# A graph network's edge loads: one transfer for each batch of a chunk, in place of one for the whole chunk

## The chip, the cores and the metric

The kernel runs on 1 core of a Trainium2 chip. The metric is the device time of one execution in microseconds; lower is better. Engines are named as in the profile: PE is TensorE (matmul), PEld its weight load, DVE is VectorE, ACT is ScalarE, POOL is GpSimd, SP is SyncE, which here only issues transfers.

## What is computed

Two layers of a graph network on 12,500 nodes of 128 features, with 200,000 edges sorted by their target node `dst`. Each layer normalizes x, sums edge attributes by target node, and adds the outcome of small dense products to x. The first layer sums 64 attributes of an edge and divides by the number of edges of the node; the second sums 128.

```python
h = jnp.maximum(_layernorm(x, axis=-1), 0.0)
# layer 0, edge_attr_64
edge_projected = edge_attr @ W_edge.T
aggregated = jax.ops.segment_sum(edge_projected, dst, num_segments=num_nodes)
aggregated = aggregated / jnp.clip(degree, 1.0)[:, None]
x = x + jnp.concatenate([h @ W_self.T, aggregated @ W_neigh.T], axis=1) @ W_final.T + b_final
h = jnp.maximum(_layernorm(x, axis=-1), 0.0)
# layer 1, edge_attr_128
agg = jax.ops.segment_sum(edge_attr, col, num_segments=x.shape[0])
x = x + jax.nn.relu(jnp.concatenate([h, agg], axis=1) @ W1 + b1) @ W2 + b2
```

## The kernel before

The edges are cut into 128 chunks of 13 x 128 (the first 32) or 12 x 128 edges (the last chunk, 127, has 832). The sum by target node is done by TensorE: for each unit of 128 edges DVE builds a one-hot matrix of 128 edges by 64 nodes (a window of nodes), and matmuls multiply the edges' attributes by it. `ring128` holds the 128 attributes of the edges, `ring64` the 64. Since `dst` is sorted and low nodes have more edges, late chunks cover more nodes than one window; so a chunk has 1, 2, 3 or 4 batches, each with a window of its own: `PARTS = (1, 2, 3, 4)` batches of `RUNS = (13, 6, 4, 3)` units, by quarter of the chunk numbers. Within a batch of R units, partition p holds R neighbouring edges, so a partition's run is R x 512 B in `ring128` and R x 256 B in `ring64`.

The work goes in ticks t = 0 to 127, one chunk each, with dense work for groups of 512 nodes between. `ORDER` lists the chunk of each tick. Chunks 15 to 20 come first. Then one from the high end (127, 126, ...) and one from the low end (21, 22, ...) take turns until tick 112. Chunks 0 to 14 come last. So two-batch chunks (32 to 63) and three-batch chunks meet four-batch chunks (96 to 127) in the middle of the run. By the order of the ticks: even ticks 6 to 68 have four batches (the first of them, chunk 127, two and a short one), odd ticks 7 to 27 one and 29 to 91 two, even ticks 70 to 92 three, ticks 93 to 112 three, and the last 15 one.

Loads go into a ring of `SLOTS = 5` slots, all of them issued by SP in the order of the ticks. SP issues the load of tick t once PE has finished the matmuls of tick t-5 (semaphore `s_mm`); PE waits at the start of tick t until the whole chunk is in the slot (semaphore `s_load[slot]`, whose target is the table `LOADED`), and for the one-hots and for free accumulators. Each transfer raises `s_load` by 16. Chunk t's last matmul is that of line 671, on which SP's waits are recorded. ACT issues the loads of x and the stores of the result on its own queue.

Of the kernel before, what the change touches and what calls it, by code (L numbers as in the profile page):

```python
# [14 lines left out]
P = 128  # L15
# [9 lines left out]
PARTS = (1, 2, 3, 4)  # L25
CH = 128
# [8 lines left out]
SLOTS = 5  # L35
# [22 lines left out]
def run_of(c):  # L58
    return RUNS[c // 32]


def first_edge(c):
    return c * 13 * P if c <= 32 else 32 * 13 * P + (c - 32) * 12 * P


def batches_of(c):


    q = c // 32
    if c == CH - 1:  # L70
        return [(0, 3, P, 0), (3, 3, P, 1), (6, 1, H, 0)]
    kinds = ((2,), (0, 1), (0, 1, 2), (0, 1, 0, 1))[q]
    return [(b * RUNS[q], RUNS[q], P, kinds[b]) for b in range(PARTS[q])]


def build_gnn(nc, x, dst, edge_attr_128, edge_attr_64, W_self, W_neigh, W_edge, W_final, b_final,
# [77 lines left out]
    for q, g in enumerate(SEQ):  # L154
        for at, other in ((FIRST_W, g + 4 if g and g in LOWER else 0), (UPPER_AT, g - 4 if g in UPPER else 0)):
            if other in (LOWER if at == FIRST_W else UPPER) and other:
                a = at + (g - 1) % 4 * GW
# [46 lines left out]
    for q in range(NG - 1, -1, -1):  # L204
        t = min(NEIGH[q] - 9, SELF[0] - 2 if SELF else CH)
# [11 lines left out]
    HOT_SUMS, ADDED, LOADED, in_slot = [0], [0], [], [0] * SLOTS  # L217
    for t, c in enumerate(ORDER):
        HOT_SUMS.append(HOT_SUMS[-1] + (2 if c >= 96 else 3))
        ADDED.append(ADDED[-1] + len(batches_of(c)))  # L220
        in_slot[t % SLOTS] += 64 if c == CH - 1 else 32
        LOADED.append(in_slot[t % SLOTS])


# [31 lines left out]
    with ExitStack() as ctx:  # L256
# [3 lines left out]
        def sem(name):  # L260
            return ctx.enter_context(nc.semaphore(name))
# [88 lines left out]
        s_load = [sem(f"s_load{i}") for i in range(SLOTS)]  # L350
# [22 lines left out]
        def otherwise(eng, general):  # L373

            eng.wait_ge(s_gen, 1)
            again = eng.value_load(gen[0:1, 0:1], min_val=0, max_val=1)
            with eng.If(again > 0):
                general()

        def every_group(eng, group):  # L380
            with eng.Fori(0, GG - 1) as g:
                group(g)
            group(GG - 1)
# [5 lines left out]
        @block.sync  # L389
        def _(sp):  # L390
            sp.wait_ge(s_dst_clear, 1)
            z0 = 32 * UNITS * P
            sp.dma_start(dst_i[0:32, :], dst[0:z0].rearrange("(r e) -> r e", r=32)).then_inc(s_dst0, 16)

            def load_edges(t):
                c = ORDER[t]
                slot, e0, R = t % SLOTS, first_edge(c), run_of(c)
                if t >= SLOTS:
                    sp.wait_ge(s_mm, t - SLOTS + 1)
                nb = 2 if c == CH - 1 else PARTS[c // 32]  # L400
                e1 = e0 + nb * R * P
                for ring, feats in ((ring128, edge_attr_128), (ring64, edge_attr_64)):
                    sp.dma_start(ring[:, slot, 0:nb * R, :].rearrange("p (b r) f -> p b (r f)", b=nb),
                                 feats[e0:e1, :].rearrange("(b p r) f -> p b (r f)", p=P, r=R)).then_inc(s_load[slot], 16)
                    if c == CH - 1:
                        sp.dma_start(ring[0:H, slot, 6, :], feats[e1:E, :]).then_inc(s_load[slot], 16)

            load_edges(0)
            for r0, r1, e0, w in ((96, 126, first_edge(96), 12 * P), (126, 127, first_edge(126), 12 * P),
                                  (127, 128, first_edge(127), LAST_E), (32, 96, z0, 12 * P)):  # L410
                sp.dma_start(dst_i[r0:r1, 0:w], dst[e0:e0 + (r1 - r0) * w].rearrange("(r e) -> r e", e=w)).then_inc(s_dst, 16)
            rest = 12 * P - LAST_E
            sp.dma_start(dst_i[127:128, LAST_E:12 * P], dst[E - rest:E].rearrange("(r e) -> r e", r=1)).then_inc(s_dst, 16)
            for t in range(1, CH):
                load_edges(t)
            sp.wait_ge(s_store, 16 * (NG + 1))

            def general():
                sp.dma_start(gen_dst_i, dst.rearrange("(p e) -> p e", p=GP)).then_inc(s_gdst, 16)

                def group(g):
                    with sp.Fori(0, PASSES) as w:
                        with sp.Fori(0, GC) as c:
                            sp.wait_ge(s_gmm, (g * PASSES + w) * GC + c + 1)
                            for ring, feats in ((gen_r128, edge_attr_128), (gen_r64, edge_attr_64)):
                                sp.dma_start(ring, feats.rearrange("(p c r) f -> p c (r f)", p=GP, r=GR)[
                                    :, bass.ds(c, 1), :].rearrange("p o f -> p (o f)")).then_inc(s_gload, 16)
                    sp.wait_ge(s_gst, g * 32 + 32)
                    if not isinstance(g, int):
                        rows = x[bass.ds(g * GW, GW), :].rearrange("(j p) f -> p j f", p=P)  # L430
                        sp.dma_start(x0[:, 0:2, :], rows[:, 0:2, :]).then_inc(s_gx, 16)
                        sp.dma_start(x0[:, 2:4, :], rows[:, 2:4, :]).then_inc(s_gx, 16)
                        sp.wait_ge(s_gstep, g * GSTEPS + GSTEPS + 1)
                        rows = out[bass.ds(g * GW, GW), :].rearrange("(j p) f -> p j f", p=P)
                        sp.dma_start(rows[:, 0:2, :], x0[:, 0:2, :]).then_inc(s_gst, 16)
                        sp.dma_start(rows[:, 2:4, :], x0[:, 2:4, :]).then_inc(s_gst, 16)
                    else:
                        n0 = g * GW
                        sp.dma_start(x0[:, 0, :], x[n0:n0 + P, :]).then_inc(s_gx, 16)
                        sp.dma_start(x0[0:LAST_N, 1, :], x[n0 + P:N, :]).then_inc(s_gx, 16)  # L440
                        sp.wait_ge(s_gstep, g * GSTEPS + GSTEPS + 1)
                        sp.dma_start(out[n0:n0 + P, :], x0[:, 0, :]).then_inc(s_gst, 16)
                        sp.dma_start(out[n0 + P:N, :], x0[0:LAST_N, 1, :]).then_inc(s_gst, 16)
                        sp.wait_ge(s_gst, g * 32 + 64)

                every_group(sp, group)

            otherwise(sp, general)
# [928 lines left out]
```

## Time and profile before

| | |
|---|---|
| runs | 531.97, 534.71, 535.15 us, median 534.71 |
| the profiled execution | 538.03 us, of which 536.2 us are the span of its instructions |
| PE, PEld busy | 494.8 us (92%), 440.6 us (82%) |
| DVE, POOL, ACT busy | 416.8, 382.9, 178.5 us |
| moved by the DMA engines | 169.55 MB, 316 GB/s on average |
| mean granted clock of TensorE | 0.978 |

The profile is of one execution of its own, so sums on it are made against 538.03 us, and the difference of the span, 1.8 us, lies outside the first and the last instruction. Busy times are shares of the span. A DMA share is that of the 16 engines, and can pass 1 where the times of packets overlap.

### The profile page before, as it was taken

What the parts mean: (1) busy time and instruction counts of PE and PEld (TensorE: products, weight loads), DVE (VectorE), ACT (ScalarE), POOL (GpSimd) and SP (SyncE); (2) the same over time, 40 slices, a digit from 0 to 9 for tenths busy, and PEclk for the clock granted to TensorE, in tenths of its full rate; (3) what the DMA queues carried; (4) which work ended last, traced back from release to release, by engine and by line L of the source; (5) the groups of instructions that cost most, each with busy time, mean ns of one, the idle gap of its engine ahead of it and who ended that gap; (6) DMA issues with size and microseconds to landing.
All of it is one profiled execution on the core that took longest, in us unless ns stands there. A gap on an engine that the chain in (4) does not pass through costs nothing.

```text
span 536.2 us, 26042 instructions
## 1 busy us (share of the span) xinstructions
PE 494.8 (92%) x10913; PEld 440.6 (82%) x10913; DVE 416.8 (78%) x1403; ACT 178.5 (33%) x397; POOL 382.9 (71%) x523
## 2 busy tenths in 40 slices
PE   8999788899989989989999999999999899999995
PEld 7889788798867878878887888789787788888784
DVE  5848989779994769978899679989969789956422
ACT  0011024243524234542525242534433362312201
POOL 2799586878696764897778977697975585863820
PEclk9997999999997989999999999999999899999998
DMA  8998999999995999999999999999999899987801
GB/s 280 398 363 293 377 372 353 364 325 363 334 329 188 343 345 299 361 312 321 368 343 381 300 343 328 377 322 316 366 339 326 278 337 325 315 306 264 335 23 33
DMA packets 113231, 169.55 MB, mean 316 GB/s; under 512 B 5486, under 2 KB 84310, under 8 KB 113111
## 3 DMA queue, kind: packets, MB, share of 16 engines
q1 hardware_dynamic: 85843, 154.42, 82.3%
q10 hardware_dynamic: 27268, 13.43, 8.7%
q8 instruction: 88, 1.44, 1.1%
q14 instruction: 32, 0.26, 0.1%
HBM read 161.43 MB, written 6.40 MB: 313 GB/s over the span
## 4 chain that ended last, share of the span: by engine, by line
PE 75%; DVE 10%; issue 9%; POOL 4%; DVEq 1%; ACT 0%; ACTq 0%; POOLq 0%
PE ps L644 25%; PE ps L662 14%; PE ps L646 5%; PE ps L731 5%; PE ps L710 5%; PE ps L722 4%; PE ps L691 4%; PE ps L682 4%; PE ps L724 3%; DVE agg L1080 2%; DVE onehot L1050 2%; POOL hot_sum L530 2%; POOL hot_part L530 1%; PE ps L583 1%; PE ps L596 1%
## 5 line engine op out<-in xcount | busy, mean ns | idle before, releaser
L644 PEld LDWEIGHTS ps<-onehot,ring 128*64 128x64 f32 x3126 | 194.6, 139 | 32.0 <-issue 25.6
L644 PE MATMUL ps<-onehot,ring 128*64 128x64 f32 x3126 | 213.3, 225 | 6.9 <-issue 6.3
L646 PE MATMUL ps<-onehot,ring 128*64 128x64 f32 x3126 | 213.8, 225 | 6.3 <-issue 6.1
L646 PEld LDWEIGHTS ps<-onehot,ring 128*64 128x64 f32 x3126 | 194.8, 139 | 7.6 <-issue 7.6
L530 POOL TENSOR_TENSOR hot_part<-onehot 128x384 bf16<-128x384 f32 (+2 forms) x128 | 118.0, 922 | 113.9 <-DVE onehot L1050 110.9
L1050 DVE TENSOR_TENSOR onehot<-iota_win,rel 128x384 f32<-128x384 f32 (+3 forms) x192 | 168.8, 880 | 0.2
L1080 DVE TENSOR_TENSOR agg<-ps,agg 128x128 f32 (+1 forms) x319 | 94.8, 297 | 85.2 <-PE ps L671 61.0
L662 PE MATMUL ps<-onehot,ring 128*64 128x64 f32 x3126 | 120.4, 224 | 7.6 <-issue 7.4
L662 PEld LDWEIGHTS ps<-onehot,ring 128*64 128x64 f32 x3126 | 107.9, 140 | 7.7 <-issue 7.4
L530 POOL TENSOR_TENSOR hot_sum<-hot_part 128x128 bf16<-128x128 bf16 x96 | 52.9, 551 | 7.5
L897 ACT ACTIVATE hn<-x,nmr,rstd 128x128 f32<-128x128 f32 x98 | 40.3, 483 | 19.9 <-DVE nmr L1142 19.9
L952 ACT ACTIVATE hid<-ps,b_col 128x512 f32<-128x512 f32 (+1 forms) x25 | 16.9, 678 | 90.0 <-PE ps L724 90.0
L508 POOL TENSOR_TENSOR x<-x,b_bc 128x512 f32<-128x512 f32 (+1 forms) x25 | 33.8, 1352 | 13.2 <-ACT h L937 13.2
L937 ACT ACTIVATE h<-x,nmr,rstd 128x128 f32<-128x128 f32 x98 | 40.4, 484 | 7.8 <-DVE nmr L1194 7.7
L731 PE MATMUL ps<-w,hid 128*128 128x128 f32 x196 | 30.4, 300 | 8.2 <-ACT own L912 5.7
L530 POOL TENSOR_TENSOR hot_sum<-hot_sum,hot_part 128x128 bf16<-128x128 bf16 x64 | 34.3, 536 | 5.0
L516 POOL MEMSET agg<- 128x1536 f32 (+2 forms) x26 | 35.4, 1364 | 2.7 <-PE ps L724 2.7
L495 POOL TENSOR_TENSOR x<-x,b_bc 128x512 f32<-128x512 f32 (+1 forms) x25 | 37.1, 1485 | 0.0
L912 ACT COPY own<-ps 128x512 f32<-128x512 f32 (+1 forms) x25 | 14.4, 577 | 64.2 <-PE ps L691 47.4
L731 PEld LDWEIGHTS ps<-w,hid 128*128 128x128 f32 x196 | 25.5, 202 | 10.2 <-issue 7.8
L710 PEld LDWEIGHTS ps<-w_c,agg 128*128 128x128 f32 x248 | 31.0, 196 | 3.1 <-issue 2.9
L502 POOL TENSOR_TENSOR x<-x,own 128x512 f32<-128x512 f32 (+1 forms) x25 | 33.5, 1339 | 0.0
(127 smaller groups left out, 648.5 us busy)
## 6 DMA issues: line engine op xcount, KB each, us to landing
ring<-in_edge_attr_dram SPq DMA_DIRECT2D x95, 768.0 KB, 5.5
ring<-in_edge_attr_dram SPq DMA_DIRECT2D x96, 384.0 KB, 7.1
ring<-in_edge_attr_dram SPq DMA_DIRECT2D x32, 832.0 KB, 5.9
ring<-in_edge_attr_dram SPq DMA_DIRECT2D x32, 416.0 KB, 7.6
x<-in_x_dram ACTq DMA_DIRECT2D x23, 256.0 KB, 7.1
out_dram<-x ACTq DMA_DIRECT2D x23, 256.0 KB
x<-in_dst_dram SPq DMA_DIRECT2D x1, 384.0 KB
x<-in_dst_dram SPq DMA_DIRECT2D x1, 208.0 KB, 3.5
```

What stands on the lines that cost most here:

```text
L495: nc.gpsimd.tensor_tensor(rows, rows, b0_bc[:, :].unsqueeze(1).to_broadcast([P, nt, D]), ALU.add).then_inc(s_xb, 1)
L516: nc.gpsimd.memset(agg[:, :, a:b], 0.0).then_inc(s_zero, 1)
L530: nc.gpsimd.tensor_tensor(out, a, b, ALU.add).then_inc(s_hotsum, 1)
L644: nc.tensor.matmul(bank[0:H, o:o + WIN], ring128[0:K, slot, u, 0:H], hots, start=u == 0, stop=r == R - 1, skip_group_check=True)
L646: nc.tensor.matmul(bank[H:P, o:o + WIN], ring128[0:K, slot, u, H:D], hots, start=u == 0, stop=r == R - 1, skip_group_check=True)
L662: nc.tensor.matmul(bank[feats, o:o + WIN], ring64[0:K, slot, u, :], onehot[0:K, hot, u, :], start=False, stop=True, skip_group_check=True)
L710: last = nc.tensor.matmul(ps_nb[:, j // 2, j % 2, :], agg[:, 1 + k, a + j * P:a + (j + 1) * P], w_c[:, k, :], start=i == 0, stop=i == len( ...
L731: last = nc.tensor.matmul(ps_row[:, j * D:(j + 1) * D], hid[:, j * P:(j + 1) * P], w2[:], start=True, stop=True)
L897: last = nc.scalar.activation(hn[:, j, :], x0[:, j0 + j, :], ACT.Relu, bias=nmr1[:, u, j:j + 1], scale=rstd1[:, u, j:j + 1])
L937: last = nc.scalar.activation(h2[:, j, :], x0[:, j0 + j, :], ACT.Relu, bias=nmr2[:, u, j:j + 1], scale=rstd2[:, u, j:j + 1])
L1050: made = nc.vector.tensor_tensor(onehot[:, t % HOTS, a:b, :], iota_win[:, :].unsqueeze(1).to_broadcast([P, b - a, WIN]), rel[:, c // 32, a ...
L1080: nc.vector.tensor_tensor(here, ps[:, t % BANKS, o:o + w * WIN].rearrange("p (a n) -> p a n", a=w), here, ALU.add).then_inc(s_added, 1)
```

## The change

`load_edges` used to issue one transfer for each of the two rings of a chunk, whose access pattern went over the partition, the batch and the run. Now it issues one for each batch. Each covers 128 partitions by one run. The runs and their places are the same, and so are the bytes. The targets of `s_load` grow with the count of transfers. Nothing is changed on PE, DVE, ACT or POOL: PE still waits for the whole chunk.

```diff
     for t, c in enumerate(ORDER):
         HOT_SUMS.append(HOT_SUMS[-1] + (2 if c >= 96 else 3))
         ADDED.append(ADDED[-1] + len(batches_of(c)))
-        in_slot[t % SLOTS] += 64 if c == CH - 1 else 32
+        in_slot[t % SLOTS] += 32 * (3 if c == CH - 1 else PARTS[c // 32])
         LOADED.append(in_slot[t % SLOTS])
...
                 e1 = e0 + nb * R * P
                 for ring, feats in ((ring128, edge_attr_128), (ring64, edge_attr_64)):
-                    sp.dma_start(ring[:, slot, 0:nb * R, :].rearrange("p (b r) f -> p b (r f)", b=nb),
-                                 feats[e0:e1, :].rearrange("(b p r) f -> p b (r f)", p=P, r=R)).then_inc(s_load[slot], 16)
+                    for b in range(nb):
+                        a = e0 + b * R * P
+                        sp.dma_start(ring[:, slot, b * R:(b + 1) * R, :].rearrange("p r f -> p (r f)"),
+                                     feats[a:a + R * P, :].rearrange("(p r) f -> p (r f)", p=P, r=R)).then_inc(s_load[slot], 16)
                     if c == CH - 1:
                         sp.dma_start(ring[0:H, slot, 6, :], feats[e1:E, :]).then_inc(s_load[slot], 16)
```

SP's instructions in the middle of the run, for a chunk of four batches, one of two, and the first load of the next one of four (the sizes are partitions, batches and elements of a run), before:

```order
L403 DMA ring128<-in_edge_attr_128_dram 128x4x384
L403 DMA ring64<-in_edge_attr_64_dram 128x4x192
L403 DMA ring128<-in_edge_attr_128_dram 128x2x768
L403 DMA ring64<-in_edge_attr_64_dram 128x2x384
L403 DMA ring128<-in_edge_attr_128_dram 128x4x384
```

and now:

```order
L405 DMA ring128<-in_edge_attr_128_dram 128x384 x4
L405 DMA ring64<-in_edge_attr_64_dram 128x192 x4
L405 DMA ring128<-in_edge_attr_128_dram 128x768 x2
L405 DMA ring64<-in_edge_attr_64_dram 128x384 x2
L405 DMA ring128<-in_edge_attr_128_dram 128x384 x4
```

Each transfer over several batches has become as many transfers in a row, at the same place in SP's order, behind the same wait for the slot. At the start, SP's instructions for chunk 127, chunk 21 and the first load of chunk 126, before:

```order
L403 DMA ring128<-in_edge_attr_128_dram 128x2x384
L406 DMA ring128<-in_edge_attr_128_dram 64x128
L403 DMA ring64<-in_edge_attr_64_dram 128x2x192
L406 DMA ring64<-in_edge_attr_64_dram 64x64
L403 DMA ring128<-in_edge_attr_128_dram 128x1664
L403 DMA ring64<-in_edge_attr_64_dram 128x832
L403 DMA ring128<-in_edge_attr_128_dram 128x4x384
```

and now:

```order
L405 DMA ring128<-in_edge_attr_128_dram 128x384 x2
L408 DMA ring128<-in_edge_attr_128_dram 64x128
L405 DMA ring64<-in_edge_attr_64_dram 128x192 x2
L408 DMA ring64<-in_edge_attr_64_dram 64x64
L405 DMA ring128<-in_edge_attr_128_dram 128x1664
L405 DMA ring64<-in_edge_attr_64_dram 128x832
L405 DMA ring128<-in_edge_attr_128_dram 128x384 x4
```

The chunks of one batch keep their two transfers. The other engines have the same instructions in the same order.

## Rows read from the trace of the kernel before

**Rows 1.** The page: span, busy time of engines, busy tenths by slice.

```profile
span 536.2 us, 26042 instructions
PE 494.8 (92%) x10913; PEld 440.6 (82%) x10913; DVE 416.8 (78%) x1403; ACT 178.5 (33%) x397; POOL 382.9 (71%) x523
PE   8999788899989989989999999999999899999995
```

**Rows 2.** The page: the chain that ended last, by engine.

```profile
PE 75%; DVE 10%; issue 9%; POOL 4%; DVEq 1%; ACT 0%; ACTq 0%; POOLq 0%
```

**Rows 3.** Waits of all engines: us in total, times, longest us.

```profile
POOL hot_part L530 <- DVE onehot L1050: 110.9, 78, 9.1
ACT hid L952 <- PE ps L724: 90.0, 24, 10.7
DVE agg L1080 <- PE ps L671: 61.0, 46, 4.6
...
PEld ps L644 <- issue: 25.6, 61, 2.8
...
PEld ps L724 <- issue: 12.0, 48, 0.5
```

**Rows 4.** Waits of SP over the run, same columns.

```profile
SPq L403 <- PE ps L671: 367.6, 123, 10.8
```

**Rows 5.** Timeline of SP, 5 to 9.2 us: start, us, what.

```profile
5.32 3.97 SPq L403 DMA_DIRECT2D ring<-in_edge_attr_dram  x8
```

**Rows 6.** The page: issues of loads onto the ring, KB each, us to landing.

```profile
ring<-in_edge_attr_dram SPq DMA_DIRECT2D x95, 768.0 KB, 5.5
ring<-in_edge_attr_dram SPq DMA_DIRECT2D x96, 384.0 KB, 7.1
ring<-in_edge_attr_dram SPq DMA_DIRECT2D x32, 832.0 KB, 5.9
ring<-in_edge_attr_dram SPq DMA_DIRECT2D x32, 416.0 KB, 7.6
```

**Rows 7.** Line 403: all issues (ns min/median/max), landing; then landing in 110:270 and 361:441.

```profile
L403 SPq DMA_DIRECT2D ring<-in_edge_attr_dram x256: 327/432/1842, 2.1 to 501.5; - x128
DMA to landing us min/median/max: 4.5/6.2/17.7
...
DMA to landing us min/median/max: 4.5/6.0/8.5
...
DMA to landing us min/median/max: 4.9/6.4/10.4
```

**Rows 8.** Line 403, windows 56:58, 59:62, 71:73, 74:76: issues; landing of the first two.

```profile
L403 SPq DMA_DIRECT2D ring<-in_edge_attr_dram x2: 340/386/433, 56.5 to 56.9; - x2
DMA to landing us min/median/max: 7.8/8.6/9.4
L403 SPq DMA_DIRECT2D ring<-in_edge_attr_dram x2: 379/879/1379, 59.6 to 60.0; - x2
DMA to landing us min/median/max: 8.5/9.1/9.7
L403 SPq DMA_DIRECT2D ring<-in_edge_attr_dram x2: 341/386/432, 71.5 to 71.9; - x2
L403 SPq DMA_DIRECT2D ring<-in_edge_attr_dram x2: 379/444/508, 74.6 to 75.0; - x2
```

**Rows 9.** Waits of SP in windows 29:110, 110:270, 270:361 and 361:441.

```profile
SPq L403 <- PE ps L671: 61.2, 21, 4.9
SPq L403 <- PE ps L671: 122.1, 41, 10.8
SPq L403 <- PE ps L671: 66.0, 23, 4.2
SPq L403 <- PE ps L671: 58.9, 20, 4.7
```

**Rows 10.** The page: DMA queues, packets, MB, share of 16 engines (q1 SP, q10 ACT).

```profile
q1 hardware_dynamic: 85843, 154.42, 82.3%
q10 hardware_dynamic: 27268, 13.43, 8.7%
q8 instruction: 88, 1.44, 1.1%
```

**Rows 11.** Windows: busy of each engine, then granted clock, DMA share, GB/s.

```profile
13.00:27.00 14.00, 12.98 (x276) 11.82 (x270) 11.62 (x21) 0.37 (x1) 11.13 (x13) 1.00 1.04 398
...
62.00:83.00 21.00, 17.55 (x492) 16.66 (x493) 19.22 (x58) 4.65 (x10) 14.66 (x19) 1.00 1.04 374
110.00:270.00 160.00, 149.92 (x3349) 132.58 (x3343) 133.50 (x481) 64.88 (x143) 120.18 (x136) 0.97 0.96 324
270.00:361.00 91.00, 87.88 (x1959) 76.36 (x1959) 79.39 (x279) 37.50 (x83) 73.52 (x90) 1.00 0.99 343
361.00:441.00 80.00, 74.08 (x1692) 66.40 (x1690) 66.30 (x247) 33.45 (x76) 58.41 (x79) 0.98 0.99 326
```

**Rows 12.** The page: DMA packets by size.

```profile
DMA packets 113231, 169.55 MB, mean 316 GB/s; under 512 B 5486, under 2 KB 84310, under 8 KB 113111
```

## The prediction

> **What bounds the kernel now.** I read the page's first part and its chain, then the waits, then what SP does, then the DMA engines. TensorE is busy 494.8 of 536.2 us, 92%, and it works in every slice of the span [rows 1]. The chain of work that ended last runs through PE for 75%, and through no transfer by name; 9% is "issue", time in which the profile shows nothing waited for [rows 2]. The list of waits says the same from the other side. The largest entries are engines that wait for PE; PE's own large entries are "issue", 25.6 us in 61 pieces at line 644 [rows 3]. SP, which issues the loads, waited 367.6 us for PE's last matmul of a chunk, in 123 pieces, which is the 128 chunks less the five that start with free slots [rows 4]. So each load stands ready before its slot is free, and the ring of five is full: PE sets the pace and the loads follow.
>
> How far are the loads ahead? In the steady stretches one transfer lands a median 6.0 to 6.4 us after its issue [rows 7]. The slot of chunk t is freed by chunk t-5 and wanted four chunks later. SP's 123 waits lie between 9.3 us [rows 5] and 501.5 us [rows 7], 4.0 us for each chunk, so four are 16 us; the second transfer is issued half a microsecond after the first and lands in a median 7.1 to 7.6 us [rows 6], which leaves 8 to 9 us. The tightest place among chunks that the change touches or that follow one is near 57 us. Chunk 15, issued at 56.5 and 56.9, lands its last part 9.4 us after the second issue, at 66.3. The issue at 71.5 is that of chunk 19, which PE's end of chunk 14 releases, so PE takes up chunk 15 at about 71.3 [rows 8]. The load is 5.0 us early. The same reading at chunk 16 is 60.0 + 9.7 = 69.7 against the issue at 74.6 that the end of chunk 15 releases: 4.9 us, or more if PE has other work between [rows 8]. The first six chunks, where data is tightest, have one batch each and are not changed.
>
> **The change part by part.** Bytes, descriptor lengths, slots, and what PE waits for stay. Only the number of issues changes. Four-batch chunks take 8 issues in place of 2, three-batch ones 6, two-batch ones 4. The description speaks of 716 transfers in place of 256; the order of the instructions has 636 at the line that had 256, and the two for the short batch stay, so 638 in place of 258, 380 more.
>
> (a) *SP's time.* Eight issues in a row at the start take 3.97 us, 0.50 each [rows 5]; the median over all is 0.43, the longest 1.84 [rows 7]. I take 0.50. 380 x 0.50 = 190 us, against 367.6 us that SP spends waiting [rows 4]. By stretch, in order: 29 to 110 us has 21 chunks and 66 more issues, 33 us against 61.2 of waiting; 110 to 270 has 41 chunks and 162 more, 81 us against 122.1; 270 to 361 has 23 and 70 more, 35 against 66.0; 361 to 441 has 20 and 80 more, 40 against 58.9; after that none [rows 9]. Everywhere SP keeps time over; least in the last, 19 us. In 110 to 270 the issue would have to cost 0.50 + 41/162 = 0.75 us before SP is the bound. Against that stand the long issues of up to 1.84 us; no row says what lengthens them. If each of the 88 packets of instruction fetch [rows 10] held SP for 1 us, that would be 88 us over the run, some 26 of the 41 left in that stretch. The room shrinks and doesn't close. All of this lies beside PE's work: cost on the path 0.
>
> (b) *Latency of a chunk.* The last transfer of a four-batch chunk is issued 7 x 0.50 = 3.5 us after the first, in place of 0.5: at most 3.0 us later. The data can't come faster than the engines move it: a chunk of 1,152 KB takes 1.18 MB / 374 GB/s = 3.2 us [rows 11], and transfers that are issued early fill that time. So most of the 3.0 us is hidden by the movement itself. Bounds are 0 and 3.0 us, and another 1.0 us for a long issue: 4.0 against 5.0 us of lead at the tightest place. I take 1 us. Cost on the path 0; if the cover were gone, each of the 54 such chunks would cost PE what is missing.
>
> (c) *The DMA engines.* Each transfer seems to add one small packet on each of the 16 engines. The page's 5,486 packets under 512 B for some 325 transfers fit that (16 x 325 = 5,200) [rows 12]. 380 x 16 = 6,080 more packets. No row has such a packet's time. From above it is the mean on the queue of the edges, 0.823 x 16 x 536.2 / 85,843 = 82 ns; nearer is the mean of the other queue, nearly all 512 B, 0.087 x 16 x 536.2 / 27,268 = 27 ns [rows 10]. By 27 ns it is 6,080 x 27 / 16 = 10 us of each engine, by 82 ns 31 us, and 0 from below. A gain is possible there as well, since a transfer now reads one unbroken piece of memory. The room is this: a backlogged stretch, 62 to 83 us, moved 374 GB/s, and the loaded stretches move 324, 343 and 326 [rows 11]. Room: 13% of 160 us, 8% of 91 and 13% of 80, together 21 + 8 + 10 = 39 us for the 312 issues added there, 0.12 us each on all engines at once. I take 0.03 (27 ns, one packet on each engine in parallel), and 0.08 is the upper end: 25 us of the 39. Hidden, cost 0.
>
> Sum: 536.2 + 0 + 0 + 0 us of span, and 538.03 of the profiled run. The median of the runs shown is 534.71, 0.6% below it; the change adds nothing to either. I put **535 us**.
>
> **A rule that speaks against the change.** One could fear that the delay from issue to landing, 4.5 us at least [rows 7], is paid by each transfer in turn; 380 x 4.5 = 1,710 us more would be the price. But the 256 of now would then take 256 x 4.5 = 1,152 us, twice the span. Landings overlap, and this rival has under 1%, counted with R1. The Trainium skill (DMA: Bandwidth & Descriptors, Bandwidth, the part on measured HBM to SBUF) advises transfers of at least 1 MiB for three quarters of the peak; its fit for transfers issued from GpSimd (Anatomy of one DMA) has about 2.0 us fixed and the bytes at 436 GB/s. By that fit, paid in turn, 380 transfers more would be 760 us, an estimate from that page; and by the advice the four-batch chunks' 192 KB would be far too small. The trace, with transfers of 384 to 832 KB that move 374 GB/s [rows 6, 11], does not show such a loss.
>
> **The rivals.** *R1, the feed falls behind (slower).* Each transfer's end costs the 16 engines a bubble. Below 0.12 us nothing is seen, above it the 312 issues of the loaded stretches each add what is over. At 0.15 us that is 9 us, 544; at 0.20 us 25 us, 560. For it: DMA's share stands at 0.96 to 1.04 in these stretches and loads move at 87 to 92% of the best rate [rows 11]. Against it: at 13 to 27 us the engines move 398 GB/s with two transfers for each chunk, share 1.04, so no idle time between transfers shows [rows 11]. Chance 9%.
> *R2, SP becomes the bound (slower).* It decides at 0.75 us for an issue. At 0.80 us the 162 issues added between 110 and 270 us, and the 80 between 361 and 441 us (limit 0.50 + 19/80 = 0.74), overrun by 8 and some 5 us: 548. For it: long issues of 1.84 us. Against: median 0.43 [rows 7]. Chance 4%.
> *R3, PE's stalls shrink (faster).* The "issue" pieces of PE, 25.6 us and 12.0 at lines 644 and 724 [rows 3], may be instruction fetch that queues on the same engines behind the edges [rows 10]. If shorter transfers let it through in half the time, 19 us go: 516. Against: the edges' packets keep their number and their size, so a fetch meets the same queue of bytes. Chance 5%.
>
> **How the numbers follow.** A measurement of this kernel can tell about 1% from no change; its own three runs span 0.6%. The forecast, nothing within 1%, has 82%: 530 to 540. R1 and R2 together give slower by over 1% 13%, R3 faster 5%. The likeliest gives 535. For 8 in 10 the range takes in the forecast's own 531 to 540 and the near end of R1 (0.14 to 0.15 us for each transfer, 542): 530 to 542.
>
> **What would show it.** In the profile of the changed kernel: SP's wait for PE falls from 367.6 to 130 to 190 us and stays some 120 pieces (steps a); if it falls below 60 us or to few pieces in 361 to 441, R2 is at work. The median of one issue stays 0.37 to 0.50 us. Packets rise by about 6,080, all of them under 512 B, and the share of the edges' queue by 0 to 3 points (step c). PE busy stays at 494 to 496 us, with the same "issue" pieces, some 35 us. R1 would show PE idle at line 644 at the first unit of a chunk, released by a transfer onto the ring; R3 would show the "issue" pieces of line 644 at half. The prediction is wrong if a wait of PE for the ring shows up in the chain, or if the "issue" share moves from 9% by over 2 points.

## The result and the profile after

The changed kernel took 528.79 us in the median of 6 runs, against 534.85 us of 6 runs of the kernel before. The ratio is 0.987, with a 95% interval of 0.983 to 0.991. In a second comparison it was 0.992 (0.988 to 0.995), 12 runs against 30. Ratios and intervals, here and below, compare only runs within 1.5% of the fastest of their kernel; medians are of all runs. No change was forecast; the kernel is about 1% faster, 4 to 7 us.

The profiled execution took 528.21 us, span 526.3. First the page of the changed kernel: span, busy times, packets, queues, the chain by engine.

```profile
span 526.3 us, 26422 instructions
PE 490.7 (93%) x10913; PEld 436.8 (83%) x10913; DVE 416.2 (79%) x1403; ACT 179.0 (34%) x397; POOL 389.6 (74%) x523
DMA packets 119314, 169.60 MB, mean 322 GB/s; under 512 B 11566, under 2 KB 90390, under 8 KB 119191
q1 hardware_dynamic: 91923, 154.44, 83.6%
PE 67%; DVE 15%; issue 10%; POOL 5%; DVEq 1%; ACT 1%; POOLq 0%; ACTq 0%
```

The packets come first: the edges' queue has 6,080 more, and as many more are under 512 B [rows 10, 12], as step (c) has it (the other 3 are packets of instructions). The edges' queue took 0.836 x 526.3 = 440.0 us of packet time, before 0.823 x 536.2 = 441.3 [rows 10]: so many more small packets cost the engines no time that shows. The chain still runs through no transfer.

Next SP: its waits over the run, then in the windows 29:108, 108:264, 264:354 and 354:430, which hold nearly the same ticks as those of [rows 9], and all issues of the loads.

```profile
SPq L405 <- PE ps L673: 124.2, 70, 6.1
...
SPq L405 <- PE ps L673: 21.7, 10, 4.7
SPq L405 <- PE ps L673: 18.9, 16, 6.1
SPq L405 <- PE ps L673: 21.4, 22, 2.9
SPq L405 <- PE ps L673: 5.6, 6, 1.4
...
L405 SPq DMA_DIRECT2D ring<-in_edge_attr_dram x636: 327/432/2278, 2.1 to 491.9; - x159
DMA to landing us min/median/max: 2.4/4.6/17.6
```

SP waited for PE for two thirds of the span, and now waits for a quarter of it. In the three-batch stretch it is nearly full: 5.6 us of waiting are left of 58.9. It waits for PE in 70 chunks, no longer in 123; in the other 53 the slot was free before SP came to it. Each issue added took (367.6 - 124.2)/380 = 0.64 us of its waiting, although the median issue is still 0.43; without the 10 us by which the span is shorter it is 0.61.

The lead at chunk 15, the tightest place among the chunks from the sixth on: SP's issues between 59 and 60 us (the last one at 59.6 is chunk 15's), their landing, and PE's last matmuls of chunk 14.

```profile
L405 SPq DMA_DIRECT2D ring<-in_edge_attr_dram x3: 431/432/1315, 57.8 to 59.6; - x3
DMA to landing us min/median/max: 5.4/5.7/7.7
...
L673 PE MATMUL ps<-hot_sum,ones_h x4: 192/194/196, 69.1 to 69.2; 128*64 128x64 bf16 x4
```

The load lands at 59.6 + 7.7 = 67.3 and is wanted from 69.2 on: 1.9 us are left of 5.0 [rows 8]. On the clock of the span it lands 1.0 us later than before, and PE is there 2.1 us sooner. Measured from the end of chunk 10, which frees the slot, it lands after 11.7 us in place of 9.9, since SP is still at the eight issues of chunk 14 and comes to chunk 15 only 3.5 us after the slot is free.

Where did PE's time come from? These are the matmul groups of the scatter lines of the changed kernel: busy us, mean ns, then idle time before them.

```profile
L648 PE MATMUL ps<-onehot,ring 128*64 128x64 f32 x3126 | 214.0, 225 | 5.3 <-issue 5.2
L646 PE MATMUL ps<-onehot,ring 128*64 128x64 f32 x3126 | 213.5, 225 | 5.6 <-issue 5.0 <-DVE onehot L1052 0.6
L664 PE MATMUL ps<-onehot,ring 128*64 128x64 f32 x3126 | 119.7, 224 | 3.7 <-issue 3.6
```

And the same of the kernel before:

```profile
L646 PE MATMUL ps<-onehot,ring 128*64 128x64 f32 x3126 | 213.8, 225 | 6.3 <-issue 6.1
L644 PE MATMUL ps<-onehot,ring 128*64 128x64 f32 x3126 | 213.3, 225 | 6.9 <-issue 6.3 <-DVE onehot L1050 0.6
L662 PE MATMUL ps<-onehot,ring 128*64 128x64 f32 x3126 | 120.4, 224 | 7.6 <-issue 7.4
```

"Issue" idle at these three lines is 13.8 us in place of 19.8. A second trace of the changed kernel has 15.0, one of the kernel before 21.3. So some 6 us of the 10 us of span are pieces in which PE waits for nothing named. PE's busy time is 4.1 us shorter too; the granted clock is 0.985 against 0.978 in the two traces. But in the second comparison the mean clock over the runs that enter the ratio is 0.985 for both kernels, so the clock's part is put down to the chance of the two executions, and the 10 us between the spans overstate the gain.

What such a piece looks like in the kernel before: the chain of waits from 192 us on, and the queues in 191.5:194.

```profile
192.25 0.29 PE ps L662 x8
192.54 2.50 issue
195.04 0.51 PE ps L662 x7
...
q1 hardware_dynamic: 655, 0.65, 77.8%
q10 hardware_dynamic: 437, 0.22, 29.2%
q8 instruction: 1, 0.02, 2.7%
```

PE stops in the middle of a chunk's row of like matmuls, whose data is all there. In that window a packet of instructions is under way on engines whose share sums to over 1. One such place proves little, but the records of the traces settle it. Number all instructions of PE in order of time, weight loads and the sequencer's own included. Then every one of PE's "issue" pieces of over 0.3 us comes at the same place of a block of 256 instructions: 20 of 20 here, and 413 of 413 in the 19 traces of this document. All but one of the 413 end 1.0 to 1.9 us after the end of one of the 88 packets of 16 KB on the queue q8 (88 blocks of 256 are 22,528 instructions, and the trace has 22,091 of PE), where a time picked at random would lie in about 15% of cases. So in these pieces PE waits for its next block of instructions, which comes over the same 16 engines as the edges. They sum to 23.8 us in this trace and 27.0 in a second one of the kernel before, against 16.9 and 16.8 in the two of the changed kernel.

### The profile page after: what moved, and what is told of

Its sections match the earlier page's. It is cut to its first block, busy times and chain, and to the rows that moved or that the text cites. A ratio compares the mean times of both kernels' runs of the same rounds, so it can differ in the third digit from the quotient of the medians.

```text
span 526.3 us, 26422 instructions
## 1 busy us (share of the span) xinstructions
PE 490.7 (93%) x10913; PEld 436.8 (83%) x10913; DVE 416.2 (79%) x1403; ACT 179.0 (34%) x397; POOL 389.6 (74%) x523
## 4 chain that ended last, share of the span: by engine, by line
PE 67%; DVE 15%; issue 10%; POOL 5%; DVEq 1%; ACT 1%; POOLq 0%; ACTq 0%
PE ps L646 23%; PE ps L664 13%; PE ps L648 4%; PE ps L733 4%; PE ps L712 4%; PE ps L724 4%; PE ps L693 4%; DVE agg L1082 3%; PE ps L726 3%; PE ps L684 3%; POOL hot_sum L532 3%; DVE onehot L1052 2%; POOL hot_part L532 2%; PE ps L598 1%; DVE x L1174 1%
## 5 line engine op out<-in xcount | busy, mean ns | idle before, releaser
L532 POOL TENSOR_TENSOR hot_part<-onehot 128x384 bf16<-128x384 f32 (+2 forms) x128 | 121.4, 949 | 99.4 <-DVE onehot L1052 93.3
L532 POOL TENSOR_TENSOR hot_sum<-hot_part 128x128 bf16<-128x128 bf16 x96 | 55.6, 579 | 7.5
L899 ACT ACTIVATE hn<-x,nmr,rstd 128x128 f32<-128x128 f32 x98 | 40.3, 482 | 19.2 <-DVE nmr L1144 19.2
L733 PE MATMUL ps<-w,hid 128*128 128x128 f32 x196 | 28.5, 288 | 7.3 <-ACT own L914 6.1
L712 PE MATMUL ps<-w_c,agg 128*128 128x129 f32 x248 | 32.3, 277 | 0.0
```

The lines of the kernel that those rows point to most:

```text
L532: nc.gpsimd.tensor_tensor(out, a, b, ALU.add).then_inc(s_hotsum, 1)
L712: last = nc.tensor.matmul(ps_nb[:, j // 2, j % 2, :], agg[:, 1 + k, a + j * P:a + (j + 1) * P], w_c[:, k, :], start=i == 0, stop=i == len( ...
L733: last = nc.tensor.matmul(ps_row[:, j * D:(j + 1) * D], hid[:, j * P:(j + 1) * P], w2[:], start=True, stop=True)
L899: last = nc.scalar.activation(hn[:, j, :], x0[:, j0 + j, :], ACT.Relu, bias=nmr1[:, u, j:j + 1], scale=rstd1[:, u, j:j + 1])
```

## The experiments

Each kernel was timed against the kernel before on the chip of its group; ratios have 95% intervals. The diffs show the lines that carry the idea, against the kernel before or, where the text says so, the changed one; the targets of `s_load` and the places from which PE reads follow them.

### The changed kernel and the kernel before, once more

No edits. 

> The changed kernel once more, for its ratio on this chip beside the three variants and for a second trace. If the gain is real, 0.983 to 0.991 of the kernel before, and PE's idle pieces of over 0.25 us sum to less than the 33 us of before. If the gain was the chance of one placement on a chip, 0.995 to 1.005.

> The kernel before, unchanged, against itself: 0.997 to 1.003 under every theory. Its trace shows how far PE's stalls and the times at the lower clock differ from one execution to the next; if its span and stalls differ from those of the first trace by as much as the changed kernel's did (10 us and 6 us), the two traces alone can't name a cause.

The changed kernel measured 0.992 (0.988 to 0.995), the kernel before against itself 1.002 (0.998 to 1.006). The gain is real; the two comparisons leave it at about 1%. Single executions of the kernel before took 531 to 544 us in this group, so a span of one trace says little by itself.

### SP's timing without the cut

```diff
                     sp.dma_start(ring[:, slot, 0:nb * R, :].rearrange("p (b r) f -> p b (r f)", b=nb),
                                  feats[e0:e1, :].rearrange("(b p r) f -> p b (r f)", p=P, r=R)).then_inc(s_load[slot], 16)
+                    for _ in range(nb - 1 if c < CH - 1 else 1):
+                        i = filled[0]
+                        filled[0] += 1
+                        sp.dma_start(filler[0:1, i:i + 1], b2[i % P:i % P + 1].rearrange("(o f) -> o f", o=1)).then_inc(s_filler, 16)
```

> The kernel before, its loads whole, and behind each load over several batches as many transfers of 4 bytes (to an unused tile) as the changed kernel has more transfers there. SP's timing is then about that of the changed kernel, with second loads 1.5 to 2 us later, but no load is cut. Theory timing (it is enough that SP hands out loads later and less in bursts): 0.985 to 0.995. Theory cut (the smaller or unbroken transfer itself helps): 0.997 to 1.005. Idle pieces of PE put down to issue: 17 to 19 us by the first, 23 to 28 us by the second.

Measured 0.998 (0.995 to 1.002). Later second loads and a fuller queue of SP, with the loads whole, bring nothing that shows. SP's timing was copied only in part: the short fillers left it 242.9 us of waiting in 117 pieces, against 124.2 in 70 in the changed kernel.

```diff
                 if t >= SLOTS:
-                    sp.wait_ge(s_mm, t - SLOTS + 1)
+                    sp.wait_ge(s_mm, t - SLOTS + 2)
```

> The kernel before with SP's wait made one chunk stricter: the load of tick t is issued when chunk t-4 is done, so transfers stay whole and large, but come one chunk later. Theory lead (the loads were too early and crowded out other transfers): 0.985 to 0.995. Theory spacing: no change in how the bytes are portioned, 0.997 to 1.003. Theory feed (loads are needed as early as they can be): lead falls from 8 to 4 us, and near tick 12 to 18 to some 1 us, so 1.00 to 1.01.

Measured 0.997 (0.994 to 1.0004). By the middle value a third of the gain could lie in the lead; the interval allows anything from none to 0.6%. A slot that is refilled one chunk later costs nothing that shows: PE waited for a load once, 0.7 us.

### How much the traffic of the edges costs PE

This kernel leaves out the loads of `ring64` after the fifth tick:

```diff
-        in_slot[t % SLOTS] += 64 if c == CH - 1 else 32
+        in_slot[t % SLOTS] += (64 if c == CH - 1 else 32) // (1 if t < SLOTS else 2)
...
-                for ring, feats in ((ring128, edge_attr_128), (ring64, edge_attr_64)):
+                for ring, feats in ((ring128, edge_attr_128), (ring64, edge_attr_64))[:2 if t < SLOTS else 1]:
```

> The kernel before without the loads of ring64 after the first five ticks (those matmuls then read what the first five left there, so the sums of the 64 attributes are not those of the reference). A third of the edges' bytes go. If PE's stalls come from the traffic of the edges: issue idle of PE from 24 to 27 us to below 15, ratio 0.96 to 0.985. If they don't depend on the traffic: issue idle stays, ratio 0.995 to 1.0.

Measured 0.976 (0.972 to 0.981). Its scatter lines, and its windows 75:160 and 300:440 with granted clock, DMA share and GB/s at the end:

```profile
L646 PE MATMUL ps<-onehot,ring 128*64 128x64 f32 x3126 | 212.1, 225 | 0.6 <-issue 0.6
L644 PE MATMUL ps<-onehot,ring 128*64 128x64 f32 x3126 | 212.0, 225 | 2.7 <-issue 1.3 <-DVE agg L1080 0.8 <-DVE onehot L1050 0.6
L662 PE MATMUL ps<-onehot,ring 128*64 128x64 f32 x3126 | 116.5, 222 | 0.7 <-issue 0.7
...
75.00:160.00 85.00, 75.51 (x1751) 68.68 (x1748) 72.29 (x270) 33.36 (x75) 68.64 (x76) 0.96 0.72 231
300.00:440.00 140.00, 136.54 (x3126) 121.52 (x3123) 128.67 (x457) 60.93 (x135) 116.52 (x146) 1.00 0.77 242
```

"Issue" idle at the three lines falls from 19.8 to 2.6 us, with the same matmuls in the same order, and PE waits for no load in either kernel. So PE's unnamed stalls depend on the traffic. They are the price of a DMA share near 1, paid although every load is early. The records show where: from PE's entry into a block of 256 instructions to the start of the packet that brings the next one, 1.2 us pass in the mean, in place of 2.5 in the kernel before. The changed kernel recovers a third to a half of the 2.4%.

### Which part of the cut

Only `ring128` was cut by batch, `ring64` left whole (against the changed kernel):

```diff
+                    if ring is ring64:
+                        sp.dma_start(ring[:, slot, 0:nb * R, :].rearrange("p (b r) f -> p b (r f)", b=nb), ...)
-                    for b in range(nb):
+                    for b in range(nb if ring is ring128 else 0):
```

> Only the loads of ring128 are cut by batch, those of ring64 stay whole: 190 of the 380 more transfers, with two thirds of the bytes cut. If the gain goes with the bytes that are cut, two thirds of it: 0.992 to 0.996. If with the number of issues, half of it. If the short transfers of ring64 matter most, 0.997 to 1.0.

Measured 0.994 (0.991 to 0.998), 0.6% of the 0.8 to 1.3%: half of the gain and two thirds of it can't be told apart.

Two transfers in place of up to four, with `PIECES = {1: ((0, 1),), 2: ((0, 1), (1, 2)), 3: ((0, 1), (1, 3)), 4: ((0, 2), (2, 4))}`:

```diff
+                    for b0, b1 in PIECES[nb]:
+                        a0, a1 = e0 + b0 * R * P, e0 + b1 * R * P
+                        sp.dma_start(ring[:, slot, b0 * R:b1 * R, :].rearrange("p (b r) f -> p b (r f)", b=b1 - b0),
+                                     feats[a0:a1, :].rearrange("(b p r) f -> p b (r f)", p=P, r=R)).then_inc(s_load[slot], 16)
```

> Chunks of two, three and four batches are cut into two transfers for each ring (the second of three batches and both of four hold two batches): 194 more transfers in place of 380, each of half a chunk. Theory size with a smooth effect: halves get more than half of the gain, 0.992 to 0.995. Theory addresses: only two-batch chunks become unbroken, a third of the bytes cut, 0.996 to 0.998. If a transfer of half a chunk is small enough: 0.990 to 0.992.

Measured 0.997 (0.994 to 1.000). By the middle value the cut in halves gets less than half of the gain.

The changed kernel, with the one-batch chunks cut too:

```diff
+                    if c < 32:
+                        of = feats[e0:e1, :].rearrange("(p r) f -> p r f", p=P)
+                        for r0, r1 in ((0, 7), (7, 13)):
+                            sp.dma_start(ring[:, slot, r0:r1, :], of[:, r0:r1, :]).then_inc(s_load[slot], 16)
```

> The changed kernel, and the chunks of one batch are cut too, into 7 and 6 units over all partitions: 94 transfers more, packets of 3,584 and 3,072 bytes in place of 6,656. Theory size: those 47 chunks have the largest transfers left, 832 KB; with the same gain for them as for the others, 0.985 to 0.989 against the kernel before, some 0.3 to 0.4% below the changed kernel. Theory addresses: such a cut reads broken pieces, so no gain on the changed kernel: 0.990 to 0.993. If SP's extra issues cost something at the start, up to 0.5% above the changed kernel.

Measured 0.991 (0.987 to 0.994), as the changed kernel. Halving the largest transfers adds nothing that can be told. (There are 32 chunks of one batch, so 64 more transfers and not the 94 of the expectation.)

### Is it the unbroken piece of memory?

A chunk read as one unbroken run for each partition, in two transfers:

```diff
-                    sp.dma_start(ring[:, slot, 0:nb * R, :].rearrange("p (b r) f -> p b (r f)", b=nb),
-                                 feats[e0:e1, :].rearrange("(b p r) f -> p b (r f)", p=P, r=R)).then_inc(s_load[slot], 16)
+                    sp.dma_start(ring[:, slot, 0:nb * R, :].rearrange("p u f -> p (u f)"),
+                                 feats[e0:e1, :].rearrange("(p u) f -> p (u f)", p=P)).then_inc(s_load[slot], 16)
```

> Two transfers for each chunk as before, but each partition takes one unbroken run over all batches, so the transfer reads one unbroken piece of memory in longer packets; units then hold other edges than the tables say, and the sums are not those of the reference. Theory addresses (an unbroken piece is served faster): 0.983 to 0.992, as the changed kernel or better, since packets are longer too. Theory size (what helps is that a transfer is small): 0.996 to 1.003.

Measured 0.992 (0.989 to 0.996), as much as the change. That speaks for the addresses as the cause, but its packets are longer as well:

```profile
DMA packets 64590, 169.53 MB, mean 320 GB/s; under 512 B 5486, under 2 KB 31702, under 8 KB 64471
```

The next three part the two. First the changed kernel, with small transfers over broken pieces:

```diff
+                    of = feats[e0:e1, :].rearrange("(p u) f -> p u f", p=P)
+                    for b in range(nb):
+                        sp.dma_start(ring[:, slot, b * R:(b + 1) * R, :], of[:, b * R:(b + 1) * R, :]).then_inc(s_load[slot], 16)
```

> The same number of transfers, the same packets and the same 128 partitions for each transfer as in the changed kernel, but a partition's 12 units lie in one unbroken run and each transfer takes a share of every such run: it reads 128 pieces with gaps between them (as a whole, the transfers of a chunk read the same piece). Units hold other edges than the tables say, so the sums are not the reference's. Theory unbroken piece for each transfer: no gain, 0.996 to 1.004. Theory size of a transfer: 0.988 to 0.993. Theory distance (what costs is the step of 192 to 384 KB between the pieces of a partition): 0.988 to 0.993 too.

> The cut into small transfers over broken pieces once more. If 0.984 was right: 0.980 to 0.989, better than the changed kernel; if it is the same effect as in the changed kernel: 0.988 to 0.993. Above 0.996 the first reading was chance, and unbroken pieces are back.

Measured 0.984 (0.976 to 0.992, four runs) and 0.986 (0.982 to 0.990, six runs); by the medians of all runs it is 0.988 both times. Then the whole unbroken chunk in packets of the old lengths (slots of 16 units, a gap of one after each part):

```diff
+                        sp.dma_start(ring[:, slot, 0:nb * (R + 1), :].rearrange("p (b r) f -> p b r f", b=nb)[:, :, 0:R, :],
+                                     feats[e0:e1, :].rearrange("(p b r) f -> p b r f", p=P, b=nb)).then_inc(s_load[slot], 16)
```

> Two transfers for each chunk and packets of the old lengths, but each partition reads one unbroken run over all batches (its parts are written with a gap of a unit between them, in slots of 16 units); the sums are not the reference's. Theory unbroken or distance: 0.988 to 0.994. Theory packets' length (that the gain of the whole unbroken transfer came from its longer packets) or theory size: 0.997 to 1.003.

Measured 1.002 (0.997 to 1.007), and 1.007 by the medians of all runs. Last the old pattern with another distance between pieces:

```diff
+                    q = 136 if c != CH - 1 else P
...
-                                 feats[e0:e1, :].rearrange("(b p r) f -> p b (r f)", p=P, r=R)).then_inc(s_load[slot], 16)
+                                 feats[e0:e0 + nb * R * q, :].rearrange("(b q r) f -> q b (r f)", q=q, r=R)[0:P]).then_inc(s_load[slot], 16)
```

> The transfers of before, but the pieces of a partition's batches lie 136 in place of 128 partition runs apart: 204 KB in place of 192, 408 in place of 384, 272 in place of 256 for the 128 attributes. It reads some edges of the next chunk, so the sums are not the reference's. If the round distance costs: 0.990 to 0.995. If any distance does: 0.997 to 1.003.

Measured 1.000 (0.996 to 1.004). The theory of addresses falls by all three. The first two of these kernels put the same bytes of memory into the same units, in packets of the same lengths, over the same 128 partitions. They differ in the number of transfers, 638 or 258, and so in the order of the packets, and in the gaps within a slot, which only the second has. The two together are worth 1.6 to 1.8%, and by the intervals at least some 0.5%. The changed kernel against the kernel before, 0.8 to 1.3%, is the same comparison without the gaps.

### How many packets one transfer holds

The kernels that gained most have in common 8 packets for each transfer on each of 16 engines (128 partitions, one packet each, if they are dealt out evenly); in the others it is 16 to 32. To test it, whole transfers in two runs of 6 units, 16 packets each:

```diff
+                        sp.dma_start(ring[:, slot, 0:14, :].rearrange("p (b r) f -> p b r f", b=2)[:, :, 0:6, :],
+                                     feats[e0:e1, :].rearrange("(p b r) f -> p b r f", p=P, b=2)).then_inc(s_load[slot], 16)
```

> Two transfers for each chunk, each partition in two runs of 6 units (packets of 3,072 and 1,536 bytes, 16 on each engine for each transfer; slots of 16 units with a gap; the sums are not the reference's). Theory packets of one transfer on one engine: between 8 (0.984 to 0.992) and 24 to 32 (1.00), so 0.994 to 0.998. Theory bytes of one transfer: no gain, 0.998 to 1.003. Theory length of the packets: most of the gain, 0.991 to 0.994.

Measured 0.993 (0.986 to 0.999), but on 4 of 12 runs; over all twelve the median is 536.93 us against 535.84. This settles nothing: the interval touches what each of the three theories expects.

### Cuts by partition

As many transfers as in the changed kernel, but each takes neighbouring partitions, 64, 48 or 32 of them:

```diff
+                    to = ring[:, slot, 0:nb * R, :].rearrange("p (b r) f -> p b (r f)", b=nb)
+                    of = feats[e0:e1, :].rearrange("(b p r) f -> p b (r f)", p=P, r=R)
+                    for p0, p1 in SHARES[nb]:
+                        sp.dma_start(to[p0:p1], of[p0:p1]).then_inc(s_load[slot], 16)
```

> As many transfers as in the changed kernel, but each chunk is cut by partitions (shares of 64, 48 or 32), and each transfer still goes over all batches, so it reads pieces from several places of the memory. Theory spacing (SP hands out the same bytes in more, smaller portions, so fewer are queued on the engines): 0.983 to 0.991, as the changed kernel. Theory addresses (a transfer that reads one unbroken piece is served faster by the memory): 0.997 to 1.003.

Measured 1.264 (1.258 to 1.270), which neither theory had. The same with every fourth partition for four batches and every second for two and three (`to[p0:P:step]`):

> Chunks cut into shares of the partitions again, but each share takes every second or every fourth partition, so that each transfer spreads over all partitions; 4 shares for four batches, 2 for two and three. Each transfer still reads pieces of all batches. If the 26% of the cut by neighbouring partitions came from the few partitions that were written at a time, this goes back to 0.98 to 1.01; if from shares of 32 partitions as such, it stays above 1.15. Where it is within 1.01: theory addresses 0.997 to 1.005, theory size of a transfer 0.985 to 0.995.

Measured 1.031 (1.026 to 1.036). The first moves 251 GB/s in 75:160 at a DMA share of 1.06, the second 317 at 0.96, where the kernel before moves 347; the last of these three lines is that of the kernel before, after one line for each cut.

```profile
75.00:160.00 85.00, 65.42 (x1356) 60.61 (x1358) 45.23 (x162) 21.81 (x49) 40.43 (x51) 0.82 1.06 251
75.00:160.00 85.00, 78.33 (x1846) 70.83 (x1844) 72.86 (x269) 32.80 (x73) 65.74 (x74) 0.98 0.96 317
75.00:160.00 85.00, 77.31 (x1847) 69.67 (x1845) 75.02 (x274) 32.08 (x72) 65.48 (x74) 1.00 1.02 347
```

In the cut by neighbouring partitions PE still waits for no load. These are its largest waits:

```profile
PE ps L666 <- issue: 40.1, 18, 4.6
PE ps L648 <- issue: 28.3, 12, 4.7
PE ps L650 <- issue: 21.5, 14, 3.6
```

All its waits of this kind of over 0.3 us, 114.9 us in 54 pieces, come at the edge of a block of instructions, and the packet with the next block starts 4.5 us after PE's entry into a block. They are 91 us more than in the kernel before, where the span grew by 131; beside them PE is busy 47 us longer, at a mean granted clock of 0.908 in place of 0.978. In the cut by stride PE really waits for loads:

```profile
PEld ps L647 <- DMA ring<-in_edge_attr_dram: 30.8, 23, 3.4
```

So a cut is only as good as the partitions that it keeps together. Neither kernel tells about size alone, since in both no transfer covers all partitions.

### More on top

```diff
                 if t >= SLOTS:
-                    sp.wait_ge(s_mm, t - SLOTS + 1)
+                    sp.wait_ge(s_mm, t - SLOTS + (2 if t >= 40 else 1))
```

> The changed kernel, with SP's wait one chunk stricter from tick 40 on, where the lead is 5 to 12 us in the changed kernel. If the small gain of the later loads (0.997) adds to that of the cut: 0.986 to 0.990. If the lead, now 1 to 8 us, is used up at some chunks: 0.993 to 1.002, and PE's waits name transfers.

Measured 0.992 (0.989 to 0.995): nothing on top of the change. Of the kernels that compute the reference, none is clearly faster than the changed one.

The table has, for every kernel, the ratio, PE's waits for instructions (its "issue" pieces of over 0.3 us, summed over a trace), and the mean time from PE's entry into a block to the start of the packet that brings the next. All are worked out from the records of the traces; where two values stand, they are from two traces.

| kernel | ratio | waits, us | to the packet, us |
|---|---|---|---|
| before | 1 | 23.8, 27.0 | 2.49, 2.49 |
| fillers | 0.998 | 20.3 | 2.56 |
| one chunk later | 0.997 | 21.7 | 2.63 |
| other distance | 1.000 | 24.9 | 2.47 |
| whole, unbroken, short packets | 1.002 | 29.9 | 2.62 |
| only `ring128` cut | 0.994 | 25.2 | 2.64 |
| cut in halves | 0.997 | 24.4 | 2.52 |
| two runs of 6 units | 0.993 | 26.0 | 2.62 |
| whole, unbroken, long packets | 0.992 | 21.9 | 2.49 |
| changed | 0.987, 0.992 | 16.9, 16.8 | 2.42, 2.41 |
| one-batch chunks cut too | 0.991 | 19.2 | 2.39 |
| small over broken pieces | 0.984, 0.986 | 18.0, 19.1 | 2.44, 2.38 |
| changed, later loads | 0.992 | 20.4 | 2.50 |
| without `ring64` | 0.976 | 2.6 | 1.21 |
| by stride | 1.031 | 22.1 | 2.43 |
| by neighbouring partitions | 1.264 | 114.9 | 4.48 |

The six traces with all loads whole and packets of the old lengths have 20.3 to 29.9 us, in the mean 24.6; the six in which every batch is a transfer of its own over all partitions have 16.8 to 20.4, in the mean 18.4. The 6 us between them are the size of the gain. Single traces scatter by several us, so the kernels between can't be placed.

## Why the prediction was wrong

**PE sets the pace, the loads are early.** Right, and still so: no transfer in the chain.

**(a) SP's time.** The kind was right, the size was not: 0.61 us for an issue in place of 0.50. By stretch, less the 2, 4, 1 and 4 us by which the stretches are shorter, it was (61.2 - 21.7 - 2)/66 = 0.57, (122.1 - 18.9 - 4)/162 = 0.61, (66.0 - 21.4 - 1)/70 = 0.62 and (58.9 - 5.6 - 4)/80 = 0.62 us. SP's wait, forecast at 130 to 190 us in some 120 pieces, was 124.2 in 70. In the three-batch stretch 5.6/80 = 0.07 us for an issue were left, so R2 deserved more weight than the text gave it. Its sign, few pieces of waiting there, did come (6 pieces), though the kernel got faster: SP nearly full is not yet SP the bound.

**(b) Latency.** Right that it costs nothing, but too small, and in part for another reason. The step took 1 us, for the later last issue of a four-batch chunk. From the freeing of the slot to the landing, the 32 chunks of four batches (the step says 54) take 9.3 us in the mean in place of 7.7, and chunk 15 takes 1.8 us longer because of SP's work on the chunk before it. Of the 3 us by which the lead fell, the other 1.2 come from PE, which gets there sooner.

**(c) The DMA engines.** 6,080 more packets on the edges' queue, as forecast. The cost taken, 0.03 us for each transfer, was too high if anything: the queue's packet time did not grow.

**The sum.** This is the step that failed: "The change adds nothing to either", built on PE's time as a constant. It isn't. PE's waits for instructions were 23.8 and 27.0 us and became 16.9 and 16.8, and the kernel without `ring64` shows 2.4% of the time hanging on the traffic of loads that are all early. R3 had named this mechanism and the direction, and got 5%. Its size, 19 us, about three times the measured gain, was taken from the wrong rows: the 25.6 and 12.0 us at lines 644 and 724 are idle time of weight loads, most of which no fetch causes, for they are still 21.9 and 12.3 us without `ring64` and 22.0 and 11.8 in the changed kernel. So its sign, the pieces of line 644 at half, did not come either, and the chain's "issue" share went from 9 to 10%: neither of these signs told of the gain. What dismissed it was one sentence: "the edges' packets keep their number and their size, so a fetch meets the same queue of bytes". The change itself and the pair of small broken (0.984, 0.986) and whole short (1.002) refute it: with number and size of the edges' packets kept, the way in which they are handed out is worth about 1%.

**What is shown and what is not.** Shown: PE's unnamed stalls are waits for the next block of instructions, and they rise and fall with the edges' traffic (2.6 us without `ring64`, 114.9 when the loads are cut by neighbouring partitions). Shown by groups of six traces, not by single ones: the cut by batch over all partitions shortens them by some 6 us. Shown: neither the unbroken reads nor the distance of pieces is needed for the gain, and a later second load or a shorter lead alone doesn't bring it. Open: why the cut helps a fetch. One reading is the count of packets of one transfer on an engine (8 against 16 to 32). The other is that portions keep the engines' queues shorter; the fillers don't test it, since they leave the large loads whole. Open too is how the whole unbroken chunk gains; by its trace its packets take less time, 0.791 x 530.4 = 419.5 us against 441.3, but its waits for instructions, 21.9 us, lie within the scatter of the kernel before. No kernel here separates these; the half-way one was too noisy.

**The rule on size.** The Trainium skill (DMA: Bandwidth & Descriptors, Bandwidth) advises transfers of 1 MiB and more. Here transfers of 96 to 384 KB in place of 384 to 768 KB made the kernel faster, and 349 GB/s were moved in 75:160 against 347 before. So this case, with many transfers in flight and each over all partitions, does not bear the rule out; transfers of 1 MiB were not tried.

## What to carry to other kernels

When the DMA engines' share is near 1, don't take an engine's time as fixed because all its loads are early: here PE's own instructions came over the same 16 engines as the loads. Look for idle that the profile puts down to nothing ("issue") on the engine itself, not on its weight loads, and try the kernel with a part of its loads left out to price it. Cutting loads by batch over all 128 partitions won 1% here; cutting them by partition lost 3 and 26%. Count an added issue at about 0.6 us of SP's time rather than at the median 0.43, and check each stretch, since the average hides that one is nearly full.

## What the hardware showed that was not expected

- Transfers onto 32 to 64 neighbouring partitions are slow: 251 GB/s at full engines in place of 347, and the whole kernel 26% longer. Every fourth or second partition costs 3%.
- In the 26% PE waits for no load. Its waits for instructions grow by 91 us, where the span grows by 131.
- PE idles some 17 us more, at three lines, with the full traffic of the edges than with two thirds of it, while waiting for none of the loads. Its pieces without a named cause all come at the same place of a block of 256 instructions and end 1.0 to 1.9 us after a 16 KB packet of instructions (412 of 413 pieces in 19 traces).
- The granted clock differs between executions of one kernel, from 0.970 to 0.992 over twelve of the kernel before, while its mean over the compared runs is the same 0.985 for both kernels.
